# Routing tokens to experts: from one pass over 98 tiles to seven groups of 14

## The reference, cut to what matters

```python
t = t + _L1_ffn_ref(_ln_t(t), gate_w, gate_b, w1, b1, w2, b2)

def _L1_ffn_ref(h, gate_w, gate_b, w1, b1, w2, b2):
    C = max(1, math.ceil(1.25 * T / E))
    logits = x @ gate_w + gate_b
    probs = jax.nn.softmax(logits, axis=-1)
    idx = jnp.argmax(probs, axis=-1)
    prb = jnp.take_along_axis(probs, idx[:, None], axis=1)[:, 0]
    one_hot = jax.nn.one_hot(idx, E, dtype=jnp.float32)
    pos = (jnp.cumsum(one_hot, axis=0) * one_hot).sum(-1).astype(jnp.int32) - 1
    kept = pos < C
    ...
    buf = zeros((E, C, D)).at[idx, pos_safe].set(x, mode='drop')
    hmid = jax.nn.relu(jnp.einsum('ecd,edf->ecf', buf, w1) + b1[:, None, :])
    ybuf = jnp.einsum('ecf,efd->ecd', hmid, w2) + b2[:, None, :]
    y_tok = ybuf[idx, pos_g] * (prb * kept)[:, None]
```

## Time and profile before

| | |
|---|---|
| median of 3 runs | 3811.91 us (3811.78 to 3816.86) |
| the profiled execution's own time | 3811.91 us |
| its span, first to last instruction | 3809.8 us |
| granted TensorE clock, mean | 0.917 |
| busy: PE, DVE, ACT, POOL | 3185.4, 2923.3, 1584.8, 839.4 us |

### The profile page before, as it was taken

The page is one execution under the profiler, slowest core; times in us unless marked ns, Lnnn a source line. Parts: engine busy times, 40 slices in busy tenths (PEclk is TensorE's granted clock), DMA queues, the critical chain, the costliest instruction groups (busy, mean ns, idle before and its releaser), DMA issues. The chain is left out here.

```text
span 3809.8 us, 40876 instructions
## 1 busy us (share of the span) xinstructions
PE 3185.4 (84%) x11501; PEld 1833.3 (48%) x11501; DVE 2923.3 (77%) x4733; ACT 1584.8 (42%) x3465; POOL 839.4 (22%) x856
## 2 busy tenths in 40 slices
PE   5999169999999999999966469999999999430797
PEld 3555135555555555555544234454454554420575
DVE  4888489999999999999959757777677674530476
ACT  1444163333343333344035366647557453110464
POOL 1455100000000000000049701121121121237255
PEclk9999689999999999999988689999999999555898
DMA  3576532121222121121045210010010000301331
GB/s 84 120 187 165 107 46 31 27 27 27 32 32 30 27 27 27 27 29 25 0 111 203 71 38 1 1 31 21 1 51 1 17 18 0 96 14 40 110 97 50
DMA packets 193545, 195.05 MB, mean 51 GB/s; under 512 B 68815, under 2 KB 164439, under 8 KB 192960
## 3 DMA queue, kind: packets, MB, share of 16 engines
q1 hardware_dynamic: 184608, 185.74, 21.6%
q0 software_dynamic: 8800, 7.70, 0.6%
HBM read 96.11 MB, written 110.92 MB: 54 GB/s over the span
## 5 line engine op out<-in xcount | busy, mean ns | idle before, releaser
L781 PE MATMUL deform_acc<-deform_prod,all_ident 128*128 128x392 f32 x4096 | 1379.4, 495 | 76.0 <-DVE deform_prod L866 70.4
L781 PEld LDWEIGHTS deform_acc<-deform_prod,all_ident 128*128 128x128 f32 x4096 | 769.5, 190 | 681.4 <-DVE deform_prod L866 177.9
L866 DVE TENSOR_TENSOR deform_prod<-deform_xw,deform_wd 128x1568 f32<-128x1568 f32 x512 | 908.6, 1786 | 19.4 <-DVE deform_wd L826 11.3
L1584 PE MATMUL attn_ps_r<-attn_prob,attn_xs 128*128 128x448 f32 (+1 forms) x1400 | 599.1, 559 | 28.9 <-POOL attn_xs L1486 28.9
L1680 ACT ACTIVATE attn_prob<-attn_ps_e,attn_nm 128x448 f32<-128x448 f32 (+1 forms) x700 | 438.1, 631 | 363.4 <-DVE attn_nm L1767 360.6
L1767 DVE TENSOR_REDUCE attn_nm<-attn_ps_e 128x1 f32<-128x448 f32 (+1 forms) x700 | 407.2, 614 | 34.6 <-PE attn_ps_e L1572 32.9
L745 ACT ACTIVATE deform_wd<-deform_zeros 128x3136 f32<-128x3136 f32 x32 | 90.1, 2815 | 808.4 <-DVE deform_prod L866 808.4
L1584 PEld LDWEIGHTS attn_ps_r<-attn_prob,attn_xs 128*128 128x128 f32 (+1 forms) x1400 | 266.3, 195 | 240.0 <-issue 178.8
L1483 POOL TENSOR_TENSOR attn_xs<-attn_xa,attn_wz 128x889 f32<-128x889 f32 (+1 forms) x100 | 166.5, 1690 | 775.9 <-DVE attn_wz L1788 775.9
L1036 POOL MEMSET rows_half<- 128x4 f32 x1 | 0.1, 101 | 1524.7 <-POOLq L67 1524.7
L1798 DVE TENSOR_TENSOR attn_xr<-attn_xr,attn_ps_r 128x448 f32<-128x448 f32 x252 | 155.7, 618 | 155.0 <-PE attn_ps_r L1584 153.9
(11 more groups left out here) (325 smaller groups left out, 4070.3 us busy)
## 6 DMA issues: line engine op xcount, KB each, us to landing
offsets_masks<-offs_om SPq DMA_DIRECT2D x56, 378.0 KB
deform_om<-offsets_masks SPq DMA_DIRECT2D x256, 82.7 KB
deform_xw<-projected SPq DMA_DIRECT2D x256, 73.5 KB
dispatched<-rows_zero SPq DMA_DIRECT2D x1, 16512.0 KB
experts_bi<-dispatched SPq DMA_DIRECT2D x32, 516.0 KB, 5.5
projected<-offs_zero SPq DMA_DIRECT2D x13, 680.0 KB
projected<-offs_zero SPq DMA_DIRECT2D x15, 544.0 KB
projected<-offs_zero SPq DMA_DIRECT2D x27, 272.0 KB
```

The lines of the kernel that those rows point to most:

```text
L781: mm = pe.matmul(out, ident[:, :], prod[:, s % NPROD, i, :], start=False, stop=(s == NCHUNK - 1 and i == NXH - 1))
L866: nc.vector.tensor_tensor(prod[:, s % NPROD, :, :].rearrange("p d (y x c) -> p d y x c", y=BY, x=UX), x, spread(w.rearrange("p (d y x) -> ...
L1584: mm = pe.matmul(ps_r[n % 2][:, 0:BK], xs[0:rows, at + i, j, :], prob[0:rows, at + i, j * BK:(j + 1) * BK], start=(i == 0), stop=(i == len ...
```

## The change

`route_stage` is rewritten; nothing else changes. The 98 tiles are seven groups of RG = 14. Tile f now holds tokens f*128 to f*128+127, so a group holds 1792 tokens that come one after another, and a group's places need only the counts of the groups before it (`before`). SP issues all seven loads at once. The normed rows are written straight into `rows`. Within a group the places come from matmuls: a triangular matrix of ones for the lower partitions of the same tile, a full matrix of ones for the groups before, and thirteen more with the full matrix for the earlier tiles of the same group, all added up in one PSUM bank. The softmax and the slots are worked out per group, and POOL issues a group's 14 indirect DMAs (`send`) when its slots are there. No loop is left: every engine's program is written out. The order per engine:

- POOL: rstds(0), rstds(1), then for each g: send(g), rstds(g+2)
- DVE: stats(0), normalise(0), then for each g: stats(g+1), choose(g), normalise(g+1), weigh(g), place(g)
- PE: turn(0), gate(0), then for each g: turn(g+1), gate(g+1), places(g)
- ACT: turned(0), then for each g: turned(g+1), the exponential of g

The core of the diff (small buffers, semaphore names and the removed text of the old loops are left out):

```diff
-FG = 7
-NFG = NF // FG
+RG = 14
+NRG = NF // RG
...
-        tok = rows[:, :, C:2 * C]
+        hn, tok = rows[:, :, 0:C], rows[:, :, C:2 * C]
...
+        before = t.sb("before", [128, NRG + 1, E8])
+        here = t.sb("here", [128, 2, E8])
...
-                tv = t4_d.rearrange("(p f) c -> p f c", p=128)
-                for g in range(NFG):
-                    if g:
-                        sp.wait_ge(t_in, 16 * g)
-                    sp.dma_start(tok[:, g * FG:(g + 1) * FG, :], tv[:, g * FG:(g + 1) * FG, :]).then_inc(t_in, 16)
+                tv = t4_d.rearrange("(f p) c -> p f c", p=128)
+                for g in range(NRG):
+                    sp.dma_start(tok[:, part(g), :], tv[:, part(g), :]).then_inc(t_in[g], 16)
+                    if g == 0:
+                        sp.dma_start(gw[:, :], ins["L1_ffn_gate_w"]).then_inc(g_in, 16)
+                        sp.dma_start(gb[:, :], row(ins["L1_ffn_gate_b"]).to_broadcast([128, E8])).then_inc(g_in, 16)
...
-                with pool.Fori(0, NFG // 2) as i:
-                    for p in range(2):
-                        n = i * 2 + p
-                        hold(pool, agg, n + 1, own)
-                        pool.tensor_scalar(ve[:, p, :], mv[:, p, :, 1], EPS, None, ALU.add).then_inc(eps, 1)
-                        hold(pool, eps, n + 1, own)
-                        pool.tensor_tensor(rs[:, p, :], ve[:, p, :], half[:, :], ALU.pow).then_inc(rstd, 1)
-
-                pool.wait_ge(slot_ok, 1)
-                pool.wait_ge(copied, NFG + 2)
-                for f in range(NF):
-                    pool.indirect_dma_start(
-                        out=buf_d, out_offset=bass.IndirectOffsetOnAxis(ap=slots[:, f:f + 1], axis=0),
-                        in_=rows[:, f, :], in_offset=None, bounds_check=E8 * SLOTS - 1, oob_is_err=False)\
-                        .then_inc(sent, 16)
+
+                def rstds(g):
+                    p = g % 2
+                    pool.wait_ge(agg, g + 1)
+                    pool.tensor_scalar(ve[:, p, :], mv[:, p, :, 1], EPS, None, ALU.add).then_inc(eps, 1)
+                    pool.wait_ge(eps, g + 1)
+                    pool.tensor_tensor(rs[:, p, :], ve[:, p, :], half[:, :], ALU.pow).then_inc(rstd, 1)
+
+                def send(g):
+                    pool.wait_ge(slot_ok, g + 1)
+                    pool.wait_ge(wt_ok, g + 1)
+                    for f in range(g * RG, (g + 1) * RG):
+                        pool.indirect_dma_start(
+                            out=buf_d, out_offset=bass.IndirectOffsetOnAxis(ap=slots[:, f:f + 1], axis=0),
+                            in_=rows[:, f, :], in_offset=None, bounds_check=E8 * SLOTS - 1, oob_is_err=False)\
+                            .then_inc(sent, 16)
+
+                rstds(0)
+                rstds(1)
+                for g in range(NRG):
+                    send(g)
+                    if g + 2 < NRG:
+                        rstds(g + 2)
                 pool.wait_ge(sent, 16 * NF)
...
+                def turn(g):
+                    pe.wait_ge(hn_ok, g + 1)
+                    if g:
+                        pe.wait_ge(ht_ok, g)
+                    for i in range(RG):
+                        mm = pe.transpose(ps_t[:, i // 4, i % 4 * 128:(i % 4 + 1) * 128], hn[:, g * RG + i, :], ident[:, :])
                     mm.then_inc(hT, 1)
 
+                def gate(g):
+                    pe.wait_ge(ht_ok, g + 1)
+                    if g:
+                        pe.wait_ge(ex_ok, g)
+                    for i in range(RG):
+                        mm = pe.matmul(ps_l[:, i * E8:(i + 1) * E8], ht[:, g % 2, i * 128:(i + 1) * 128], gw[:, :],
                                        start=True, stop=True)
                     mm.then_inc(l_ps, 1)
 
+                def places(g):
+                    pe.wait_ge(hot_ok, g + 1)
+                    if g:
+                        pe.wait_ge(c_ok, g)
+                    h = hot[:, g % 2, :, :].rearrange("p f e -> p (f e)")
+                    n = RG * E8
+                    pe.matmul(ps_c[:, 0:n], tri[:, :], h, start=True, stop=False)
+                    pe.matmul(ps_c[:, 0:n], ones[:, :], spread(before[:, g, :], 1, RG), start=False, stop=False)
+                    for d in range(1, RG):
+                        mm = pe.matmul(ps_c[:, d * E8:n], ones[:, :], h[:, 0:n - d * E8], start=False, stop=(d == RG - 1))
+                    mm.then_inc(c_ps, 1)
+
+                turn(0)
+                gate(0)
+                for g in range(NRG):
+                    if g + 1 < NRG:
+                        turn(g + 1)
+                        gate(g + 1)
+                    places(g)
...
-                        nc.scalar.activation(rows[:, bass.ds(n * FG, FG), 0:C], hn[:, p, :, :], ACT.Copy)\
-                            .then_inc(copied, 1)
+                def turned(g):
+                    act.wait_ge(hT, g + 1)
+                    if g >= 2:
+                        act.wait_ge(l_ps, g - 1)
+                    for i in range(0, RG, 4):
+                        w = min(4, RG - i) * 128
+                        last = nc.scalar.activation(ht[:, g % 2, i * 128:i * 128 + w], ps_t[:, i // 4, 0:w], ACT.Copy)
+                    last.then_inc(ht_ok, 1)
+
+                turned(0)
+                for g in range(NRG):
+                    if g + 1 < NRG:
+                        turned(g + 1)
+                    act.wait_ge(ex_ok, g + 1)
+                    nc.scalar.activation(ex[:, g % 2, :, :], ex[:, g % 2, :, :], ACT.Exp).then_inc(exp_ok, 1)
...
-                for e in range(E8):
-                    do(nc.vector.tensor_tensor_scan(cum[:, :, e], one[:, :], hot[:, :, e], 0.0, ALU.mult, ALU.add))
...
+                def stats(g):
+                    p = g % 2
+                    dve.wait_ge(t_in[g], 16)
+                    for j in range(RG):
+                        last = nc.vector.bn_stats(st[:, p, j, :], tok[:, g * RG + j, :])
+                    last.then_inc(stat, 1)
+                    dve.wait_ge(stat, g + 1)
+                    for j in range(RG):
+                        last = nc.vector.bn_aggr(mv[:, p, j, :], st[:, p, j, :])
+                    last.then_inc(agg, 1)
+
+                def normalise(g):
+                    p = g % 2
+                    dve.wait_ge(rstd, g + 1)
+                    for j in range(RG):
+                        last = nc.vector.tensor_scalar(hn[:, g * RG + j, :], tok[:, g * RG + j, :], mv[:, p, j, 0:1],
+                                                       rs[:, p, j:j + 1], ALU.subtract, ALU.mult)
+                    last.then_inc(hn_ok, 1)
+
+                def choose(g):
+                    p = g % 2
+                    l, h = lg[:, p, :, :], hot[:, p, :, :]
+                    dve.wait_ge(l_ps, g + 1)
+                    then(nc.vector.tensor_tensor(l, ps_l[:, 0:RG * E8].rearrange("p (f e) -> p f e", e=E8),
+                                                 spread(gb[:, :], 1, RG), ALU.add))
+                    then(nc.vector.tensor_reduce(mx[:, p, :], l, AX, ALU.max))
+                    nc.vector.tensor_tensor(ex[:, p, :, :], l, spread(mx[:, p, :], 2, E8), ALU.subtract).then_inc(ex_ok, 1)
+                    if g >= 2:
+                        dve.wait_ge(c_ps, g - 1)
+                    then(nc.vector.tensor_tensor(h, l, spread(mx[:, p, :], 2, E8), ALU.is_equal))
+                    then(nc.vector.tensor_tensor(h, h, spread(less8[:, :], 1, RG), ALU.mult))
+                    then(nc.vector.tensor_reduce(idx[:, p, :], h, AX, ALU.min))
+                    then(nc.vector.tensor_scalar(idx[:, p, :], idx[:, p, :], float(E8), None, ALU.add))
+                    a = do(nc.vector.tensor_tensor(h, spread(iot[:, :], 1, RG), spread(idx[:, p, :], 2, E8), ALU.is_equal))
+                    dve.wait_ge(step, a)
+                    then(nc.vector.tensor_reduce(here[:, p, :], h.rearrange("p f e -> p e f"), AX, ALU.add))
+                    nc.vector.tensor_tensor(before[:, g + 1, :], before[:, g, :], here[:, p, :], ALU.add).then_inc(hot_ok, 1)
+
+                def weigh(g):
+                    p = g % 2
+                    dve.wait_ge(exp_ok, g + 1)
+                    then(nc.vector.tensor_reduce(sm[:, p, :], ex[:, p, :, :], AX, ALU.add))
+                    nc.vector.reciprocal(rows[:, part(g), 2 * C + 1], sm[:, p, :]).then_inc(wt_ok, 1)
+
+                def place(g):
+                    p = g % 2
+                    dve.wait_ge(c_ps, g + 1)
+                    a = do(nc.vector.tensor_tensor(cum[:, p, :, :], hot[:, p, :, :],
+                                                   ps_c[:, 0:RG * E8].rearrange("p (f e) -> p f e", e=E8), ALU.mult))
+                    dve.wait_ge(step, a)
+                    dve.sem_inc(c_ok, 1)
+                    then(nc.vector.tensor_reduce(pos[:, p, :], cum[:, p, :, :], AX, ALU.add))
+                    then(nc.vector.tensor_scalar(out_of[:, p, :], pos[:, p, :], float(CAP) + 0.5, float(DROPPED), ALU.is_gt,
```

(61 more changed lines are left out.)

121 lines of the change are left out of this document (27 added, 94 removed).

## The result

The changed kernel takes 3871.49 us at the median (3864.89 to 3872.94, 4 runs) against 3813.66 for the kernel before (3811.78 to 3816.86, 4 runs): 57.8 us longer, ratio 1.0143, 95% interval 1.0129 to 1.0158 (the two medians by themselves give 1.0152). The forecast was 3873, within 3842 to 3890. The profiled execution took 3871.03 us.

What follows compares the result with a forecast made beforehand. Bound: a route stage of two serial halves, 130.4 us routing and 125.2 issuing, 255.55 in all. New stage 54.6 + 225 + 37.1 = 317, 61 longer, so 3811.9 + 61 = 3873 us; range 3842 to 3890.

Steps and rivals of the forecast that it cites:

- The mechanism: Route stage: rstds(g+2) waits behind send(g)'s 14 issues, holding normalise, PE's work and the next slots; 61 us longer, chance 0.78.
- First slots: Start of the route stage: everything serial from the first load to group 0's place, 54.6 us.
- Cycle: Route stage, slots to slots: five equal rounds of 45 us, POOL issuing nothing in 27 of them.
- Two blocks: End of the route stage: the last two groups' sends follow without a gap, 35.8 us of issues.
- pow of 14 elements: POOL's pow in rstds for a whole group: 2.65 us, between 1.5 (no growth) and 3.0 (double).
- stats, normalise, copies: Per-group pieces: DVE's stats 4.2 us and normalise 3.8 plus 0.2, ACT's copies about 1.9 plus 0.1.
- places: PE's 15 new accumulating matmuls per group, 30 passes: 4.8 us plus 0.3, bounds 3.5 and 6.4.
- The hops: Waits from one engine's end to the next engine's start, added to each piece's price: 0.1 to 0.3 us mostly.
- Half of a gate at the high clock: Lower end of the range: PE's gates partly at 2.4 GHz, 2.7 us less a group, seven times.
- The first (POOL's arithmetic isn't held by the issues): POOL: rstds(g+2) runs while send(g) is still issued; cycle 30 us, 3798 us in total; chance 0.04.
- The second (the clock rises in every burst): PE: turn, gate and places get the high clock, 5.5 us less a cycle; 3836 us, or 3829; chance 0.10.
- The third (dearer issues): POOL's issues cost up to 0.29 us more each beside DVE or from row order: 3901 us; chance 0.06.

Runs made afterwards that it cites:

- dense numbers: Changed kernel with a group's 15 places matmuls followed by 15 more of the same shapes, streaming normed tokens instead of one-hots: 3907.66 us, ratio to before 1.0237.
- the short places: Changed kernel with only 3 of the 15 matmuls of a group's places left and slots copied from token numbers: 3839.77 us.

## Why the prediction was right

**The mechanism** came as forecast. The adds and pows stand behind the issues, DVE is released by POOL's pow, the gaps between the first six blocks are 22 to 24 us of waiting besides 3 of arithmetic (27 forecast), the last two blocks touch, and no stats waits for a load but the first. The experiments on the order show the links: with the pow early (behind the third issue), in between (behind the eighth), and with turn, gate and places taken from behind it.

**The terms** against what they measured. First slots: 54.6 forecast; the first issue came at 52.9, so the slots at 52.0. Cycle: 45 forecast, 44.0 measured. Two blocks: 35.8 forecast, 35.7 measured. pow of 14 elements: 2.65 and 2.63. stats, normalise, copies: within 0.3. Three terms were off, and that they nearly cancel is luck:
- places was taken as 4.8 us, halfway, because "wide passes close together are just where a rise would come". It measured 6.55 to 6.57 in all seven groups, the upper bound or a little over, at a granted clock of 0.50:

```profile
3311.51:3324.10 12.59, 12.54 (x58) 12.44 (x58) 0.53 (x3) 0.12 (x1) 0.00 (x0) 0.50 0.00 1
```

  That step of the prediction was wrong in its reason and cost 1.7 us a cycle.
- The hops were set at 0.1 to 0.3 each; in the cycle shown above the five from pow to place measured 0.03 to 0.05. Some 1.1 us a cycle the other way. From the slots to the first issue it was 0.8, not 1.3.
- Three of seven gates (4.67, 4.52, 4.28 us) ran partly at the high clock, the others took 6.14 with 5.99 to the next matmul. Spread over the cycles that is 0.7 us less.

The stage came out 53 us longer, against 61 in the sum. The medians differ by 57.8; the rest is in the stages ahead, whose spread over the profiles is larger than that. So the order of work and the size of a cycle were forecast, but that 3871.49 lies 1.5 us from 3873 is luck: the stage was 8 us shorter than the sum, but 4.6 us of the difference lie outside the stage, and the kernel before now has a median 1.8 us above the 3811.91 on which the sum was set.

One step of the range is miscounted. Half of a gate at the high clock is worth (5.98 - 3.26)/2 = 1.36 us, and the 2.7 of the prediction is a whole gate; with the 7.8 of places and the 6.9 of pow that makes 24 less, not 26. The measurement is far from that bound.

**The rivals.** The first (POOL's arithmetic isn't held by the issues) is excluded by the trace: the add starts where the fourteenth issue ends, five times of five. The second (the clock rises in every burst) happened in three turns of seven and in no places; with twice the transposes it happened in every turn, and even then was back down at the latest 0.2 us into places. The sentence of the Trainium skill (TensorE: Matmul & The Clock Gate, Part 4: PE-mode transpose), that the full clock does not engage for transposes, is contradicted by these runs for transposes of f32: in the kernel with 28 of them the granted clock is 1.00 from 3396 to 3397, in the middle of a turn, and in all eleven profiles transposes were the only thing in this stage behind which it rose. The third (dearer issues) is excluded: 0.985 us an issue here, 0.976 before.

## What to carry to other kernels

A pipeline is as deep as its shallowest program order. Before trusting that "the dispatch runs while the next groups are normed", write down each engine's order and ask what stands behind the long block on the engine that does the dispatch; here 3 us of arithmetic behind 18 us of issues held a whole round of DVE and PE. And the consumer should not be queued behind work that belongs to the next group: places ahead of the next turn, with the orders of ACT and DVE to match, gave 102 us, the early pow 75, and both together 135 by the medians; in the stage itself it is 97, 67 and 127.

## What the runs showed that I had not expected

- PE was busy for 18.9 us without a break, with passes up to 112 columns wide and with dense numbers, at a granted clock of 0.50; behind 14 transposes in 3.2 us it rose in three of seven groups, behind 28 in every one. The same row of 14 didn't always do it: over the nine kernels that have it the clock rose behind 14 of the 63 such rows, five of seven with the short places, none of seven in the kernel with both edits on the order and in the one with dense numbers. What decides among equal rows is open, and so is why gate and places never raised it. It isn't the number format: in the changed kernel's next stage it rose, between 3606 and 3608, behind f32 matmuls 512 columns wide (windows, columns as before):

```profile
3606.00:3608.00 2.00, 2.00 (x4) 0.73 (x4) 0.00 (x0) 1.00 (x2) 0.00 (x0) 0.64 1.03 410
3608.00:3610.00 2.00, 1.75 (x8) 0.74 (x6) 0.00 (x0) 1.66 (x4) 0.00 (x0) 1.00 0.91 363
```

- The idle time between the last issue and the next stage was 10.27 us with 98 issues (10.30 before) and 6.23 with 49; in the other kernels with 98 issues it was 10.3 to 10.8. It doesn't depend on when the issues were made: in the changed kernel 70 of them were over long before. What is done there, some 0.08 us for each, wasn't tried.
